# Two layers written out one after the other, and the last stage's constants loaded inside the last layer

## The chip, the cores and the metric

The kernel runs on one core of a Trainium2 chip. The metric is the device time of one execution in microseconds. The core has five engines that run their own instruction streams and meet only at semaphores: TensorE (PE, with its weight loads shown as PEld), VectorE (DVE), ScalarE (ACT), GpSimd (POOL) and SyncE (SP), which here issues nearly all of the transfers.

## The reference, cut to what matters

```python
x = x + gnn(layernorm(x), edge_index)            # two layers, below; 1250 nodes, 512 features
x = x + ffn(layernorm(x))                        # the last stage
# gnn, for l in range(2):
q, k, v = (x @ Wq[l].T + bq[l]) * DH**-0.5, x @ Wk[l].T, x @ Wv[l].T       # 8 heads of 64
w = softmax over the edges of each target of (q[tgt] . k[src])
x = batchnorm(x + (sum of w * v[src]) @ Wo[l].T + bo[l], g1[l], beta1[l])
x = batchnorm(x + relu(x @ W1[l].T + b1[l]) @ W2[l].T + b2[l], g2[l], beta2[l])
# after the two layers: layernorm(x, ln_g, ln_b)
# ffn: four nibbles and three flags of each row are read off, three small two-layer networks
# (160 wide; only 5 rows of w1 and one column of w2 matter) give a number from 0 to 15 for
# each of two nibbles, and a one-hot of it, times 2, is added to columns 80 to 111.
```

## The kernel before, in words

**The first stage** (up to 217 us) normalises the input, counts the edges between every pair of nodes with one-hot products, and stores the logarithm of the counts as a bias, the residual and the shifted input to HBM. It is not touched.

**The layers** are one hardware loop, `with nc.Fori(0, LAYERS) as layer` (L557), so that both run the same instructions; only the transfers use the loop's register, to find their layer's weights. A layer has three blocks, and all five engines meet at the end of each block. The first block (L621) transposes the weights and computes k, q and v. Every float32 operand of a product is split into a high part (`..._hi`, rounded to the type in which TensorE is fast) and a low part (`..._lo`, the rest), and a product is three matmuls. The second block (L743) is the attention. The third (L959) is the output projection, the normalisation `t1`, the small feed-forward network (products called `f` and `g`), and the normalisation `t2`. Its result `t2` is kept feature-major, [128, 4, 1250], so that chunk c holds 128 features.

**The end of a layer.** TensorE does the twelve `g` products (four chunks of three), and after the last of them 70 small matmuls of `keep_clock` (L1033), whose results nobody reads: they are there to keep TensorE's clock up. ScalarE copies each product from PSUM to `t2` (L1070). VectorE takes the moments (L1105, L1100, L1101), waits for ScalarE's square root (L1044), works out scale and shift in five one-column steps (`normed`, L1123 to L1127) and applies them to the chunk (L1129). Then ScalarE makes `h_hi` (L1050), GpSimd makes `h_lo` of the first three chunks (L951, called at L980) and VectorE that of the last one (L1170). `h_hi` and `h_lo` are what the next layer's projections read. SP loads the next layer's Wk at the block's start (L964) and stores each finished chunk of `t2` as the next layer's residual (L968). All of this is done in both passes of the loop, so in the last layer too, where no layer follows.

**The last stage** (L1231) is one more block. TensorE turns `t2` into ten node-major tiles of 125 nodes (L1399); six of them are normalised by VectorE's statistics (L1470), four by ScalarE's sums (L1326, L1334). VectorE multiplies by the gain (L1444), adds the shifted input `x_in2` (L1453), and normalises again. From there on VectorE reads off the nibbles, TensorE does the twenty hidden rows (L1428), and VectorE weights and sums fifteen of them (L1537) while ScalarE and GpSimd share the other five.

The constants of this stage are fetched and built inside it: `gain_all` (L1235) and `x_in2` (L1238) by SP; then one column of each `w2` as `w_out` (L1242) and one element of each `b2` as `b_out` (L1244), also by SP; five rows of `w1` and the bias as `w_in` by nine small transfers on ScalarE's queue (L1315 to L1317). GpSimd clears `w_all` (L1268) and splits `w_in` into high and low (L1277, L1279), and SP copies the two parts by sixteen small transfers into `w_all` (L1251). TensorE spreads `w_out` over all partitions with one product against ones (L1404), after the last of the ten tiles, and ScalarE copies that to `w_out_all` (L1338) after its sums of squares and before the square root of the second half.

What is in which region of SBUF sets when a constant can be loaded: `x_in2` lies where the output projection's `a_hi` was (region R1), and `w_all`, `w_out` and the others lie in regions that the attention's biases or `t1` used.

## Time and profile before

| | |
|---|---|
| time, median of 3 runs | 1246.8 us (1242.3 to 1251.4) |
| time of the profiled execution | 1250.26 us |
| its span, first to last instruction | 1248.4 us |
| mean granted clock of TensorE | 0.94 of full speed |
| PE, PEld busy | 1074.7 us (86%), 888.3 us (71%) |
| DVE busy | 785.0 us (63%) |
| ACT, POOL busy | 566.1 us (45%), 436.9 us (35%) |

The span is the time between the first and the last instruction that the profiler recorded; the device time has 1.9 us around it. The shares are means over the whole run. The stages follow each other with a meeting of all engines between them, so what ends a stage has to be read from that stage alone, from the timeline of each engine. TensorE's granted clock is at 1.0 (2.4 GHz) or 0.5 (1.2 GHz).

### The profile page before, as it was taken

How to read it: one execution, taken by the hardware profiler on the slowest of the kernel's cores; microseconds unless marked ns; L12 is line 12 of the kernel's file. 1: busy time of each engine (PE TensorE's matmuls, PEld its weight loads, DVE VectorE, ACT ScalarE, POOL GpSimd, SP SyncE). 2: the span in 40 equal slices, each digit the busy share in tenths (PEclk: the TensorE clock that was granted, in tenths of full speed). 3: DMA queues.
4: the chain of work that ended last, by engine and by line, in shares of the span. 5: the costliest groups of instructions: out<-in, count | busy, mean ns of one | idle time of the engine just before them, and what ended most of it. 6: DMA issues, size and time to landing. Idle time of an engine off the chain costs nothing. (4 is left out here: it accounts for less than half of the span.)

```text
span 1248.4 us, 20276 instructions
## 1 busy us (share of the span) xinstructions
PE 1074.7 (86%) x6736; PEld 888.3 (71%) x6737; DVE 785.0 (63%) x2449; ACT 566.1 (45%) x1034; POOL 436.9 (35%) x482
## 2 busy tenths in 40 slices
PE   4778785999589999999899699859999999989933
PEld 2545453898578888888698699648888888879821
DVE  5665563232557777777577524247777777748878
ACT  5432331210356666666524320046666666643435
POOL 5655565000244444444212200124444444302314
PEclk9888897999889999999999899889999999999965
DMA  6010124734841212213200454563121211230153
GB/s 129 21 40 20 40 90 125 179 83 93 214 100 34 55 38 51 50 34 116 76 27 21 132 124 103 104 180 79 34 54 34 63 42 34 100 101 1 62 115 85
DMA packets 58472, 96.35 MB, mean 77 GB/s; under 512 B 15874, under 2 KB 39174, under 8 KB 58128
## 3 DMA queue, kind: packets, MB, share of 16 engines
q1 hardware_dynamic: 58348, 95.19, 30.9%
q8 instruction: 52, 0.85, 0.3%
q14 instruction: 36, 0.29, 0.1%
q10 hardware_dynamic: 36, 0.01, 0.0%
HBM read 37.55 MB, written 24.17 MB: 49 GB/s over the span
## 5 line engine op out<-in xcount | busy, mean ns | idle before, releaser
L786 POOL TENSOR_SCALAR probs<-probs,mass_inv 125x1250 f32<-125x1250 f32 x160 | 210.9, 1319 | 309.2 <-DVE mass_inv L909 309.2
L805 PE MATMUL banks<-k_stack,q_stack 128*125 128x416 f32 (+1 forms) x960 | 299.2, 398 | 12.4 <-DVEq L887 12.4
L870 ACT ACTIVATE probs<-probs,neg_peak 125x1250 f32<-125x1250 f32 x160 | 213.5, 1334 | 153.7 <-DVE neg_peak L923 153.7
L900 DVE CUSTOM_DVE_ANT_0 probs<-banks,scores_bias 125x416 f32<-125x416 f32 (+1 forms) x480 | 267.6, 583 | 24.6 <-PE banks L805 20.2
L819 PE MATMUL banks<-ident,probs 125*125 125x125 f32 x1600 | 260.4, 278 | 26.0 <-POOL probs L786 19.6
L819 PEld LDWEIGHTS banks<-ident,probs 125*125 125x125 f32 x1600 | 242.9, 189 | 49.1 <-POOL probs L786 23.2
L859 ACT ACTIVATE probs_t<-banks 125x500 f32<-125x500 f32 x320 | 152.6, 477 | 130.9 <-PE banks L819 130.8
L833 PE MATMUL banks<-probs_t,v_pair 125*64 125x250 f32 x1600 | 186.2, 379 | 0.9 <-ACT probs_t L859 0.9
L805 PEld LDWEIGHTS banks<-k_stack,q_stack 128*125 128x125 f32 x960 | 147.8, 192 | 40.4 <-issue 26.4
L891 DVE COPY probs_t<-banks 125x500 f32<-125x500 f32 x160 | 108.2, 676 | 74.0 <-PE banks L819 74.0
L475 PE MATMUL banks<-onehot_src,onehot_dst 125*125 125x512 bf16 x540 | 120.5, 387 | 32.9 <-POOL onehot_dst L290 17.5
L833 PEld LDWEIGHTS banks<-probs_t,v_pair 125*64 125x64 f32 x1600 | 107.5, 136 | 54.4 <-ACT probs_t L859 1.3
L403 DVE TENSOR_SCALAR onehot_src<-iota,e_col 125x1250 bf16<-125x1250 f16 x180 | 93.9, 566 | 66.8 <-issue 34.1
L475 PEld LDWEIGHTS banks<-onehot_src,onehot_dst 125*125 125x125 bf16 x540 | 76.2, 157 | 77.5 <-issue 56.3
L290 POOL TENSOR_SCALAR onehot_dst<-own,target_col 125x125 bf16<-125x125 f16 x120 | 99.0, 840 | 8.2 <-POOL target_col L287 8.2
L607 POOL CAST q_split<-q_t 128x250 fp32r<-128x250 f32 x40 | 15.8, 395 | 239.5 <-DVE q_t L731 149.6
L951 POOL TENSOR_TENSOR h_lo<-t,h_hi 128x1250 fp32r<-128x1250 f32 x12 | 34.5, 2872 | 117.6 <-ACT h_hi L1050 117.6
L694 PE MATMUL banks<-h_hi,wt_hi 128*128 128x416 f32 (+1 forms) x192 | 69.8, 363 | 2.3 <-DVE k_lo L728 2.3
L694 PE MATMUL banks<-h_hi,wt_lo 128*128 128x416 f32 (+1 forms) x192 | 68.8, 358 | 0.0
L694 PE MATMUL banks<-h_lo,wt_hi 128*128 128x416 f32 (+1 forms) x192 | 68.7, 358 | 0.0
L907 DVE TENSOR_SCALAR mass<-mass 125x1 f32<-125x1 f32 x160 | 24.6, 154 | 69.1 <-ACT probs L870 69.1
L333 ACT ACTIVATE more<-banks 125x1250 f32<-125x1250 f32 x10 | 12.1, 1211 | 113.6 <-PE banks L480 113.6
(247 smaller groups left out, 1459.0 us busy)
## 6 DMA issues: line engine op xcount, KB each, us to landing
q_stack<-q_split SPq DMA_DIRECT2D x160, 125.0 KB, 2.4
scores_bias<-edge_bias SPq DMA_DIRECT2D x8, 1171.9 KB
edge_bias<-bias SPq DMA_DIRECT2D x10, 585.9 KB
k_stack<-k_hi SPq DMA_DIRECT2D x16, 312.5 KB, 4.6
k_stack<-k_lo SPq DMA_DIRECT2D x16, 312.5 KB, 5.6
resid<-residual SPq DMA_DIRECT2D x2, 2500.0 KB, 10.1
residual<-t SPq DMA_DIRECT2D x8, 625.0 KB, 2.9
values<-v_stage SPq DMA_DIRECT2D x2, 2400.0 KB
```

Source lines behind the costliest of these rows:

```text
L290: op = nc.gpsimd.tensor_scalar(onehot_dst[:, k, 0:NT], own[:, 0:NT], target_col[:, k:k + 1], None, ALU.is_equal)
L403: op = nc.vector.tensor_scalar(onehot_src[:, k, :], iota[:, :], e_col[:, 1, ds(first + RING * q + k, 1)], None, ALU.is_equal)
L475: last = nc.tensor.matmul(counts[par][:, s:s + w], onehot_dst[:, k, 0:NT], onehot_src[:, k, s:s + w], start=False, stop=True, skip_group_c ...
L694: mm = nc.tensor.matmul(bank[:, 0:sn], w[:, i, c * P:(c + 1) * P], h[:, i, s0:s0 + sn], **edge)
L786: nc.gpsimd.tensor_scalar(probs[:, u % 4, :], probs[:, u % 4, :], mass_inv[:, u % 4:u % 4 + 1], 1.0, ALU.mult, ALU.mult).then_inc(att["pro ...
L805: mm = nc.tensor.matmul(pb[0:NT, t % 5, 0:sn], q_stack[:, n % 2, half, part, tile * NT:(tile + 1) * NT], k_stack[:, head * N + s0:head * N ...
L819: mm = nc.tensor.transpose(pb[0:NT, 5 + t % 2, j * NT:(j + 1) * NT], probs[:, u % 4, (j0 + j) * NT:(j0 + j + 1) * NT], ident[0:NT, 0:NT])
L833: mm = nc.tensor.matmul(pb[half * DH:(half + 1) * DH, 7, 0:GN], v_pair[:, c % 2, j, half * DH:(half + 1) * DH], probs_t[:, n % 2, half, j, ...
L859: nc.scalar.activation(to, of, ACT.Copy).then_inc(att["t_free0"], 1)
L870: nc.scalar.activation(probs[:, u % 4, :], probs[:, u % 4, :], ACT.Exp, bias=neg_peak[:, u % 4:u % 4 + 1], accum_out=mass[:, u % 4:u % 4 + ...
L891: nc.vector.tensor_copy(to, of).then_inc(att["t_free1"], 1)
L900: nc.vector.tensor_tensor_reduce(out=probs[:, slot % 4, s0:s0 + sn], in0=pb[0:NT, t % 5, 0:sn], in1=scores_bias[:, (n % GROUPS) * GROUP + ...
```

## The change

1. `with nc.Fori(0, LAYERS) as layer` becomes `for layer in range(LAYERS)`: the instructions of both layers are written out. The offsets of the transfers become constants.
2. The last layer makes no `h_hi` and `h_lo`, stores no residual and loads no Wk.
3. In the last layer's third block, SP instead issues the gain, the nine transfers of `w_in` (before on ScalarE's queue, in the last stage) and the six of `w_out` and `b_out`; then waits until the output projection is done and issues the four of `x_in2`; then waits for GpSimd's split and issues the sixteen of `w_all`. GpSimd, after its low parts of the rectified values, sets the ones, clears `w_all` when `t1` is no longer read, and splits `w_in`.
4. In the last stage the product that spreads `w_out` stands ahead of tile 6 of the ten, and ScalarE's copy of it comes first of all its work there. The splits, the clearing of `w_all` and these transfers are gone from this stage. `w_all`, `w_in`, `w_in_hi` and `w_in_lo` lie at other addresses.

```diff
-        with nc.Fori(0, LAYERS) as layer:
...
+        w_all = place("w_all", [P, SET, HID], F32R, "RP")
...
+        w_in = place("w_in", [NF, HID], F32, "RV", 2048)
+        w_in_hi = place("w_in_hi", [NF, HID], F32R, "RV", 7936)
+        w_in_lo = place("w_in_lo", [NF, HID], F32R, "RL", 47872)
...
+        for layer in range(LAYERS):
+            last_layer = layer == LAYERS - 1
...
                 def _(sp):
                     clear(sp, [*att.values(), *bias_in, *v_in, *q_in, v_stored])
 
-                    sp.dma_start(w_nat[0][:, :, :], weight(gnn["Wk"], DC)[:, ds((LAYERS - 1) * DC, DC), :]).then_inc(wk_in, 16)
-
-                    for c in range(DC):
-                        sp.wait_ge(oph["t_done"], DC + 1 + c + len(pieces(c)))
-                        sp.dma_start(res_d[:, c, :], t2[:, c, :]).then_inc(res_stored, 16)
-                    sp.wait_ge(wk_in, 16)
+                    one = lambda v: v.rearrange("(a n) -> a n", a=1)
+                    if last_layer:
+                        sp.dma_start(gain_all[:, :], one(gnn["ln_g"]).to_broadcast([NT, D])).then_inc(fin["gain"], 16)
+                        for o, name in enumerate(OPS):
+                            w1, b1 = ffn[name + "_w1"], ffn[name + "_b1"]
+                            cols = slice(o * GE, (o + 1) * GE)
+                            sp.dma_start(w_in[0:2, cols], w1[0:2, :]).then_inc(fin["w"], 16)
+                            sp.dma_start(w_in[2:5, cols], w1[44:47, :]).then_inc(fin["w"], 16)
+                            sp.dma_start(w_in[5:6, cols], one(b1)).then_inc(fin["w"], 16)
+                        for o, name in enumerate(OPS):
+                            with nc.allow_non_contiguous_dma("one column of w2; one element to all"):
+                                sp.dma_start(w_out[:, o * GE:(o + 1) * GE],
+                                             ffn[name + "_w2"][:, RESULT:RESULT + 1].rearrange("n a -> a n")).then_inc(fin["w_out"], 16)
+                                sp.dma_start(b_out[:, o:o + 1], one(ffn[name + "_b2"])[:, RESULT:RESULT + 1].to_broadcast([NT, 1])).then_inc(fin["b_out"], 16)
+                        sp.wait_ge(oph["filled"], max(t for t, job in enumerate(ojobs) if job[0] == "o") + 1)
+                        for k in range(2):
+                            for rows in SPREAD:
+                                sp.dma_start(x_in2[rows, part(k), :], shifted_d.rearrange("(t p) d -> p t d", p=NT)[rows, part(k), :]).then_inc(fin[f"x{k}"], 16)
+                        sp.wait_ge(fin["w_split"], 2)
+                        sp.wait_ge(fin["consts"], 2)
+                        for q in range(SET):
+                            for k, weights in enumerate((w_in_hi, w_in_lo, w_in_hi, w_in_lo)):
+                                rows = slice(q * ROW + k * NF, q * ROW + (k + 1) * NF)
+                                sp.dma_start(f32(w_all[rows, q, :]), f32(weights[:, :])).then_inc(fin["w_all"], 16)
+                    else:
+                        sp.dma_start(w_nat[0][:, :, :], weight(gnn["Wk"], DC)[:, ds((layer + 1) * DC, DC), :]).then_inc(wk_in, 16)
+
+                        for c in range(DC):
+                            sp.wait_ge(oph["t_done"], DC + 1 + c + len(pieces(c)))
+                            sp.dma_start(res_d[:, c, :], t2[:, c, :]).then_inc(res_stored, 16)
+                        sp.wait_ge(wk_in, 16)
...
                     for n in range(3):
                         pool.wait_ge(oph["done"], ojobs.index(("f", 1, n)) + 1)
                         rectified_low(nc.gpsimd, 1, n)
-                    for c in range(DC - 1):
-                        low(pool, nc.gpsimd, c, t2, h_hi, h_lo, "h_hi", "h_lo")
-                    pool.wait_ge(oph["h_lo"], DC - 1)
+                    if last_layer:
+                        nc.gpsimd.memset(one_f[:, :], 1.0).then_inc(fin["consts"], 1)
+                        pool.wait_ge(oph["h1_lo"], DC - 1)
+                        pool.wait_ge(oph["h1_lo_last"], 2)
+                        pool.wait_ge(oph["h1_hi"], DC + 1)
+                        nc.gpsimd.memset(f32(w_all[:, :, :]), 0.0).then_inc(fin["consts"], 1)
+                        pool.wait_ge(fin["w"], 16 * 9)
+                        nc.gpsimd.tensor_copy(w_in_hi[:, :], w_in[:, :]).then_inc(fin["w_split"], 1)
+                        pool.wait_ge(fin["w_split"], 1)
+                        nc.gpsimd.tensor_tensor(w_in_lo[:, :], w_in[:, :], f32(w_in_hi[:, :]), ALU.subtract).then_inc(fin["w_split"], 1)
+                    else:
+                        for c in range(DC - 1):
+                            low(pool, nc.gpsimd, c, t2, h_hi, h_lo, "h_hi", "h_lo")
+                        pool.wait_ge(oph["h_lo"], DC - 1)
...
                             if c and n == 2:
                                 root(1, c - 1)
-                            if c > 1 and n == 2:
+                            if c > 1 and n == 2 and not last_layer:
                                 high(1, c - 2, h_hi, t2)
                             summed(c, n)
-                    high(1, DC - 2, h_hi, t2)
+                    if not last_layer:
+                        high(1, DC - 2, h_hi, t2)
                     root(1, DC - 1)
-                    high(1, DC - 1, h_hi, t2)
+                    if not last_layer:
+                        high(1, DC - 1, h_hi, t2)
...
                     normed(1, DC - 1, t2, G2, BE2)
-                    low(dve, nc.vector, DC - 1, t2, h_hi, h_lo, "h_hi", "h_lo_last")
+                    if not last_layer:
+                        low(dve, nc.vector, DC - 1, t2, h_hi, h_lo, "h_hi", "h_lo_last")
...
             @block.scalar
...
+                act.wait_ge(fin["w_out_sent"], 1)
+                nc.scalar.activation(w_out_all[:, :], pb[0:NT, 7, 0:HID], ACT.Copy).then_inc(fin["w_out_all"], 1)
                 for i in SPANS[1]:
...
                 op.then_inc(fin["first_squares"], 1)
-                act.wait_ge(fin["w_out_sent"], 1)
-                nc.scalar.activation(w_out_all[:, :], pb[0:NT, 7, 0:HID], ACT.Copy).then_inc(fin["w_out_all"], 1)
                 root(0, 1)
...
             @block.tensor
             def _(pe):
                 for i in range(TILES):
+                    if i == SPANS[1][0]:
+                        pe.wait_ge(fin["w_out"], 48)
+                        pe.wait_ge(fin["consts"], 1)
+                        nc.tensor.matmul(pb[0:NT, 7, 0:HID], one_f[:, :], w_out[:, :], start=True, stop=True).then_inc(fin["w_out_sent"], 1)
                     if i >= 7:
                         pe.wait_ge(fin["used"], i - 6)
                     for c in range(DC):
                         mm = nc.tensor.transpose(pb[0:NT, i % 7, c * P:(c + 1) * P], t2[:, c, i * NT:(i + 1) * NT], ident[:, :])
                     mm.then_inc(fin["turned"], 1)
 
-                pe.wait_ge(fin["w_out"], 48)
-                pe.wait_ge(fin["consts"], 1)
-                nc.tensor.matmul(pb[0:NT, 7, 0:HID], one_f[:, :], w_out[:, :], start=True, stop=True).then_inc(fin["w_out_sent"], 1)
                 pe.wait_ge(fin["used"], TILES)
 
```

## Rows read from the trace of the kernel before

**Rows 1.** Busy time by window: us, then each engine's busy us, PEclk, DMA share, GB/s.
```profile
217.71:702.57 484.86, 452.81 (x2976) 388.73 (x2976) 306.94 (x973) 231.50 (x414) 146.70 (x129) 0.98 0.32 79
706.50:1190.35 483.85, 452.45 (x2976) 388.39 (x2976) 306.98 (x973) 231.41 (x414) 146.54 (x129) 0.97 0.31 77
```

**Rows 2.** The chain that ended last, last stage: start us, us, what.
```profile
1201.25 10.31 DMA w_out<-in_L_ffn_xor_w
...
1211.60 1.97 PE banks L1404 x2
```

**Rows 3.** Instructions of L557 and L1127: ns least/median/most, first and last start.
```profile
L557 PEldq COMPARE_BRANCH  x2: 74/1708/3342, 703.1 to 1190.9; - x2
...
L1127 DVE SCALAR_TENSOR_TENSOR tiny<-mv,tiny,vec x16: 219/221/2506, 643.0 to 1185.6; 128x1 f32<-128x1 f32 x16
```

**Rows 4.** Timeline: the loop's way back, and the second layer's first Exp.
```profile
701.04 1.53 DVE L951 TENSOR_TENSOR h_lo<-t,h_hi 128x625 fp32r<-128x625 f32 x2 [0.28 <-ACT h_hi L1050]
...
706.43 1.28 ACT L712 ACT_TABLE_LOAD   x1 [4.81 <-issue]
706.50 3.67 PE L679 MATMUL banks<-ident,wk_nat 128*128 128x128 f32 x16 [9.43 <-issue]
...
808.23 1.35 ACT L870 ACTIVATE probs<-probs,neg_peak 125x1250 f32<-125x1250 f32 x1 [51.39 <-DVE neg_peak L923]
```

**Rows 5.** VectorE's timeline at the end of the last layer.
```profile
1173.46 2.51 DVE L1127 SCALAR_TENSOR_TENSOR tiny<-mv,tiny,vec 128x1 f32<-128x1 f32 x1
...
1180.07 2.15 DVE L1127 SCALAR_TENSOR_TENSOR tiny<-mv,tiny,vec 128x1 f32<-128x1 f32 x1
...
1185.60 1.78 DVE L1127 SCALAR_TENSOR_TENSOR tiny<-mv,tiny,vec 128x1 f32<-128x1 f32 x1
1187.42 1.12 DVE L1129 TENSOR_SCALAR t<-t,tiny 128x625 f32<-128x625 f32 x2
```

**Rows 6.** GpSimd's timeline in the last layer's third block.
```profile
1160.85 1.07 POOL L956 TENSOR_TENSOR r_lo<-r_full,r_hi 128x416 fp32r<-128x416 f32 x1 [1.09 <-DVE r_full L1157]
1173.04 2.92 POOL L951 TENSOR_TENSOR h_lo<-t,h_hi 128x1250 fp32r<-128x1250 f32 x1 [11.12 <-ACT h_hi L1050]
```

**Rows 7.** TensorE's timeline: the last layer's end, the last stage's start.
```profile
1177.02 7.82 PE L100 MATMUL banks<-ident 128*128 128x256 bf16 x70
1191.00 6.30 PE L1399 MATMUL banks<-ident,t 128*125 128x128 f32 x28 [6.17 <-PEq L959]
```

**Rows 8.** Busy time by window, columns as in rows 1: TensorE's clock.
```profile
710.00:712.00 2.00, 2.00 (x7) 1.92 (x7) 1.37 (x2) 0.60 (x1) 0.00 (x0) 0.50 1.06 367
...
1106.00:1108.00 2.00, 1.28 (x14) 0.57 (x8) 0.00 (x0) 0.38 (x1) 0.00 (x0) 1.00 0.00 0
...
1195.00:1197.00 2.00, 2.00 (x11) 2.00 (x10) 1.69 (x3) 0.00 (x0) 0.00 (x0) 0.50 1.00 185
```

**Rows 9.** VectorE's timeline in the last stage.
```profile
1192.25 0.70 DVE L1470 BATCH_NORM_STATS2 f_st<-banks 125x6 f32<-125x512 f32 x1 [1.90 <-PE banks L1399]
1193.10 0.70 DVE L1470 BATCH_NORM_STATS2 f_st<-banks 125x6 f32<-125x512 f32 x1 [0.15 <-PE banks L1399]
...
1202.47 1.06 DVE L117 TENSOR_SCALAR f_w<-f_w 125x6 f32<-125x6 f32 x1
...
1206.00 0.75 DVE L1453 SCALAR_TENSOR_TENSOR x_res<-x_res,f_w,x_in 125x512 f32<-125x512 f32 x1 [2.27 <-DMA x_in<-shifted]
...
1214.30 0.18 DVE L114 RECIPROCAL f_w<-f_w 125x4 f32<-125x4 f32 x1 [1.26 <-ACT f_w L1321]
```

**Rows 10.** GpSimd's timeline in the last stage.
```profile
1190.98 1.69 POOL L1268 MEMSET w_all<- 128x1920 f32 x1
...
1202.30 1.20 POOL L1279 TENSOR_TENSOR w_in_lo<-w_in,w_in_hi 6x480 fp32r<-6x480 f32 x1
```

**Rows 11.** SP's queue in the last stage, first and last of sixteen.
```profile
1205.06 3.95 SPq L1251 DMA_DIRECT2D w_all<-w_in_hi  x1
...
1218.94 0.66 SPq L1251 DMA_DIRECT2D w_all<-w_in_lo  x1
```

128 lines of the change are left out of this document (47 added, 81 removed).

## The prediction

> **What bounds the kernel now.** I read the windows by stage first. The two passes of the loop take 484.9 and 483.9 us with the same counts of instructions on every engine [rows 1]: 78% of the span, and the change leaves their insides alone but for the last pass's end. So the gain or loss has to come from three seams: the way back of the loop, the end of the last layer, and the last stage. For these I read the chain of waits and then each engine's timeline, because at a meeting of all engines only the latest one counts.
>
> The chain of the last stage goes through the third `w_out` transfer (10.31 us from issue to landing) and the product that spreads it, 1.97 us [rows 2]. VectorE's timeline adds what the chain doesn't show: it waits 2.27 us for `x_in2` and 1.26 us for ScalarE's root, which sits behind the copy of the spread `w_out` [rows 9]. Before the stage, VectorE holds the last layer open; TensorE ends its clock-keeping at 1177.02 + 7.82 = 1184.84 [rows 7], 5.5 us before VectorE's end at 1190.35 [rows 1].
>
> **Writing out the loop.** At the way back, TensorE's branch takes 3.34 us, at the exit, not taken, 0.07 [rows 3]. From the end of VectorE's work (701.04 + 1.53 = 702.57) to the first transpose, 706.50, it is 3.93 us [rows 4]; at the exit, from 1190.35 [rows 1] to 1191.00 [rows 7], 0.65. The difference, **3.3 us**, lies on the path: ScalarE resumes at 706.43 too, and every product of the layer follows. Which value straight code gives is not in these rows. If fetching new code is what costs, and not the branch, nothing is saved; the lower bound is 0. But the first pass is code that has never run, and it is no slower than the second by more than 1.0 us in 484 [rows 1], so I take 3.3. The upper bound adds the clock: in 710 to 712 TensorE still runs at 0.5 [rows 8], that is 1.2 GHz, at half pace since 706.50; were all of these 5.5 us at full clock, 2.75 more would be saved. I expect no such thing, as the idle stretch shortens by 3.3 us only, from 9.43 [rows 4] to about 6.1, and the one of 6.17 us in front of the last stage also ends at 1.2 GHz [rows 7, 8].
>
> The Trainium skill's page "Runtime: NRT & Kernel Launch" (Instruction fetch mechanics) says that fetching ahead is sequential, that crossing a block of code is mostly hidden, and that a taken branch out of the window waits for a fetch. By it the whole 3.3 us goes; by the branch's row alone, anything from 0 to 3.3. No run here yet shows straight code at this seam.
>
> A side effect: ScalarE reloads its function table at the start of the pass, 1.28 us, beside TensorE's first transposes. Without the loop that load can be left out there and fall in front of the first Exp. There ScalarE has been idle for 51.39 us [rows 4], so 0 is likely; if the load waits for the same semaphore as the Exp, it costs at most 2 x 1.28 = 2.6 us over both layers.
>
> **The end of the last layer.** The dropped high parts take ScalarE out of the way, and the dropped low parts take GpSimd out of VectorE's: L1127 is a one-column step of 0.22 us [rows 3], but three times it takes 2.51, 2.15 and 1.78 us [rows 5]. The first ends at 1173.46 + 2.51 = 1175.97, GpSimd's `h_lo` at 1173.04 + 2.92 = 1175.96 [rows 5, 6]: it stands still until GpSimd is done. The three excesses are 6.44 - 0.66 = 5.8 us, all in VectorE's row towards the end. VectorE's last useful step ends at 1187.42 + 1.12 = 1188.54; less 5.8 that is 1182.8. Then TensorE's 70 clock-keeping products, untouched, end last: 1184.84. The stage starts **5.5 us** earlier, not 7.5: the clock-keeping is late next.
>
> What moves in here has to fit. GpSimd is free at 1160.85 + 1.07 = 1161.9 [rows 6] and needs 1.69 for clearing `w_all` and 1.20 for the low part [rows 10]; with the small cast and the ones I put 4 us: done at 1166. VectorE may stand still for at most the 1.20 us, twelve microseconds ahead of TensorE's last real product and at a time when it waits for products anyway: 0. SP's twenty transfers ahead (gain, nine `w_in`, six `w_out` and `b_out`, four `x_in2`) go out during the output projection, where SP before issued only Wk and residuals; they are queued behind nothing that others wait for. Behind the wait for the split stand sixteen `w_all`: the first took 3.95 us, the last 0.66 [rows 11], together 3.95 + 15 x 0.70 = 14.5 us, so SP ends at 1180.5, 4.3 us ahead of TensorE. The Wk load and the four residual stores are worth 0: SP is not the last.
>
> The Trainium skill's page "SBUF — State Buffer" (SBUF: two separate sides) says that a VectorE instruction with two SBUF inputs waits for a GpSimd instruction that reads SBUF, and one with a single input outside the two-port modes never does. By it the moved cast and subtraction may meet only small steps here; the three long L1127 agree with the first half, and no row here tests the second.
>
> **The last stage.** VectorE's row is followed, with what each wait becomes:
> - The first 28 transposes take 6.30 us at 1.2 GHz, 0.225 each [rows 7, 8], and the first six statistics go at their pace: 0.85 apart (1192.25 to 1193.10) for 0.70 us of work [rows 9]. Now the idle time of TensorE before them is about half a microsecond, and across a comparable seam at 1106 to 1108, where it also stood still in part, the clock stayed at 1.0 [rows 8]. At 2.4 GHz four transposes take 0.45, so VectorE's own 0.70 is the pace: 5 x 0.15 = 0.75, 0.4 at the first one, and up to 0.4 more as neighbours overlap. I take 1.5.
> - L117 takes 1.06 us where a like step (L114) takes 0.18; it ends with GpSimd's subtraction, 1202.30 + 1.20 = 1203.50 [rows 9, 10], which has left the stage: 0.9.
> - `x_in2` has landed: 2.27 less an ordinary 0.04, 2.2.
> - The root no longer waits for `w_out`: 1.26 less 0.04, 1.2. The spreading product, 1.97 us at 1.2 GHz [rows 2], about 1.0 at full clock, now stands ahead of tile 6; ScalarE has slack, since tiles 7 to 9 wait for VectorE's multiplications anyway.
>
> Together **5.8 us**. After that VectorE works without a gap through the nibbles, the weighting and the output, and none of it changes.
>
> **The sum.** 3.3 + 5.5 + 5.8 = 14.6 us off 1250.26, the profiled execution's own time: 1235.7. That execution lies 3.5 above the median of the runs, 1246.8; off that, **1232 us**. One percent, 12.5 us, is about what a measurement can tell from no change; the line to "faster" is 1234.3.
>
> **The rivals.**
> - *Straight code stalls as the branch did.* Then only 11.3 is saved: 1235.5. For it: the code is fetched over the same transfer engines. Against: the equal passes. 0.13.
> - *SP becomes the last at the layer's end.* Its sixteen small transfers would need over (1184.8 - 1166) / 16 = 1.2 us each; at 3.95 each, as the first one, it would end 63 us after 1166, but that one stood behind much larger traffic. At 1.5 each SP ends at 1190 and the 5.5 is gone: 1237.5. 0.08.
> - *TensorE's clock has fallen at the seam after all.* The 1.5 of the first item is lost: 1233.5. 0.07.
> - *The table load lands in front of the Exps*: 1234.8. 0.06.
> - *Slower.* Written out, the last pass's code is new, where the loop had it run before. If TensorE then stands still for a branch's 3.34 us at each seam of both layers (three blocks each, six times), 20 us are added against 11.3 saved: 1255.5. It decides from the fourth such stall. The first pass's equal time speaks strongly against it. 0.04.
>
> The forecast keeps 0.62. The range takes the unknown 2.75 of the clock below, and above it the case of straight code that stalls and the SP case, with some 2 us for medians of few runs: 1227 to 1239. Faster by over 1%: nearly all of the forecast's own chance (0.57), most of the clock case and about half of the code and table cases, 0.72; within 1% 0.24; slower 0.04.
>
> **What would show it.** In the profile after: the gap between VectorE's last step of layer one and the first Wk transpose at 0.65 us rather than 3.93; no L951 in the last layer, and three L1127 of 0.22 us there; the last stage's first transpose within a microsecond of the clock-keeping's end; PEclk 1.0 during the 28 transposes and statistics about 0.62 to 0.70 apart; no wait of L1453 on a transfer; the sixteen `w_all` issues over before the clock-keeping ends. It is wrong if the layers' insides grow, if any engine other than TensorE ends the last layer, or if the clock reads 0.5 over the first tiles.

## The result, and the profile after

The changed kernel takes **1235.4 us** (median of 4 runs, 1230.3 to 1236.2) where the kernel before takes 1247.8 (4 runs, 1242.3 to 1251.4). The ratio of the runs is 0.990, with a 95% interval of 0.985 to 0.994: 12.4 us less, 1%. The forecast was 1232, so the time lies 3.4 us above it and inside the range of 1227 to 1239. The profiled execution took 1236.21 us with a span of 1234.5; against the profiled execution of before, 1250.26, that is 14.05 us less, and the forecast's sum was 14.6.

The first part of the page of the kernel after has each engine's busy time, share of the span and number of instructions:

```profile
PE 1072.8 (87%) x6736; PEld 886.3 (72%) x6737; DVE 775.1 (63%) x2447; ACT 561.2 (45%) x1029; POOL 429.4 (35%) x479
```

All five fell a little (VectorE by 9.9 us), and none of that says where 14 us of span went. As before, the seams have to be read. Busy time by window, columns as in [rows 1]: the first layer, from its first Wk transpose to VectorE's last step; the second, from its first transpose to the end of the clock-keeping; then two stretches over the first tiles of the last stage.

```profile
218.81:705.61 486.80, 453.99 (x2976) 389.15 (x2976) 306.86 (x973) 231.36 (x414) 146.53 (x129) 0.97 0.32 79
706.00:1182.80 476.80, 451.97 (x2976) 388.32 (x2976) 299.33 (x971) 226.73 (x409) 141.34 (x130) 0.98 0.33 78
1182.00:1184.00 2.00, 1.58 (x15) 1.28 (x13) 0.08 (x1) 0.00 (x0) 0.83 (x3) 1.00 0.00 0
1184.00:1188.00 4.00, 3.69 (x25) 2.67 (x24) 3.97 (x11) 0.84 (x2) 0.14 (x2) 1.00 0.00 0
```

The first layer is 486.80 us long, where it took 484.83 from the first transpose at 217.74: 1.97 more, with the same number of instructions as in [rows 1]. The last two rows have TensorE's clock at 1.00, 2.4 GHz, where [rows 8] had 0.50 in the same place.

**The loop's seam.** TensorE's timeline at the end of layer one and the start of layer two (start us, us, engine, line, instruction, and in brackets the idle time before it and what ended it); VectorE's last step of layer one stands in the fence after it:

```profile
706.00 3.65 PE L736 MATMUL banks<-ident,wk_nat 128*128 128x128 f32 x16 [6.02 <-PEq L1016]
```

```profile
704.08 1.53 DVE L1008 TENSOR_TENSOR h_lo<-t,h_hi 128x625 fp32r<-128x625 f32 x2 [0.28 <-ACT h_hi L1143]
```

704.08 + 1.53 = 705.61, so TensorE starts 0.39 us behind VectorE, where it was 3.93 [rows 4]. Its idle stretch is 6.02 us, not 9.43, and the sixteen transposes still take 3.65 us, at 1.2 GHz. Behind them the clock came back sooner than before. Busy time over the first six microseconds of layer two, the kernel before and then the kernel after:

```profile
706.50:712.50 6.00, 6.00 (x24) 5.88 (x25) 2.77 (x4) 3.61 (x5) 0.00 (x0) 0.50 1.01 337
```

```profile
706.00:712.00 6.00, 6.00 (x28) 5.95 (x29) 2.76 (x4) 2.39 (x4) 0.00 (x0) 0.66 0.64 176
```

The mean clock is 0.66 where it was 0.50: the stretch at half clock ends 4.1 us behind the first transpose, where it ended 6.0 us behind it.

**The end of the last layer.** L1127 of before is L1222 after. VectorE's timeline:

```profile
1171.42 0.22 DVE L1222 SCALAR_TENSOR_TENSOR tiny<-mv,tiny,vec 128x1 f32<-128x1 f32 x1
...
1179.42 0.22 DVE L1222 SCALAR_TENSOR_TENSOR tiny<-mv,tiny,vec 128x1 f32<-128x1 f32 x1
1179.67 1.12 DVE L1224 TENSOR_SCALAR t<-t,tiny 128x625 f32<-128x625 f32 x2
```

VectorE is done at 1180.79. GpSimd's and SP's timelines there:

```profile
1162.27 1.22 POOL L1070 TENSOR_TENSOR w_in_lo<-w_in,w_in_hi 6x480 fp32r<-6x480 f32 x1
```

```profile
1163.52 0.82 SPq L1044 DMA_DIRECT2D w_all<-w_in_hi  x1
...
1174.28 0.66 SPq L1044 DMA_DIRECT2D w_all<-w_in_lo  x1
```

SP issued its last of the sixteen at 1174.94, and TensorE, on its timeline, ends last:

```profile
1174.98 7.82 PE L100 MATMUL banks<-ident 128*128 128x256 bf16 x70
1183.21 2.86 PE L1409 MATMUL banks<-ident,t 128*125 128x128 f32 x24 [0.42 <-PEq L1016]
```

From the end of the clock-keeping, 1182.80, to the first tile it is 0.41 us; before it was 1191.00 - 1184.84 = 6.16 [rows 7].

**The last stage.** VectorE's timeline, to hold against [rows 9]:

```profile
1183.92 3.69 DVE L1477 BATCH_NORM_STATS2 f_st<-banks 125x6 f32<-125x512 f32 x6 [3.13 <-PE banks L1409]
...
1192.83 0.17 DVE L117 TENSOR_SCALAR f_w<-f_w 125x6 f32<-125x6 f32 x1
...
1193.24 0.75 DVE L1460 SCALAR_TENSOR_TENSOR x_res<-x_res,f_w,x_in 125x512 f32<-125x512 f32 x1
...
1200.18 0.17 DVE L114 RECIPROCAL f_w<-f_w 125x4 f32<-125x4 f32 x1
...
1204.57 0.19 DVE L114 RECIPROCAL f_w<-f_w 125x6 f32<-125x6 f32 x1 [0.34 <-ACT f_w L1327]
```

Six statistics run in one piece, no step waits for a transfer or for ScalarE's square root in the first normalisation, and L117 is short. From the first tile to the reciprocal of the second norm it is 1204.57 - 1183.21 = 21.36 us. The chain of waits of the kernel before has that reciprocal at 1219.04, 28.04 us behind its first tile at 1191.00 [rows 7]. From there to VectorE's last operation both kernels need the same (25.44 and 25.42).

**The accounts** of the profiled executions, by such marks in both traces:

| stretch | before | after | difference |
|---|---|---|---|
| start of the program to the first Wk transpose | 217.74 | 218.81 | +1.07 |
| layer one, to VectorE's last step | 484.83 | 486.80 | +1.97 |
| seam of the loop | 3.93 | 0.39 | -3.54 |
| layer two, to the end of the clock-keeping | 478.34 | 476.80 | -1.54 |
| from there to the first tile | 6.16 | 0.41 | -5.75 |
| last stage to the reciprocal of the second norm | 28.04 | 21.36 | -6.68 |
| the rest of the span | 29.4 | 29.9 | +0.6 |
| sum | 1248.4 | 1234.5 | -13.9 |

The three seams gave 15.97 us; 3.6 came back in places that the change does not touch, and 1.5 went there. The first stage is the least steady of all: over the fourteen profiles of this case it ends between 213.5 and 219.1 us, so that the time of a single execution says little about an edit worth 2 us. Marks inside the stage that was edited do.

Of the 0.6 us in the last row 0.5 is no scatter. From VectorE's last step to the end of the span it is 3.45 us in the kernel before and 3.98 in the kernel after, and 3.4 to 3.5 or 3.9 to 4.0 in every other profile, the larger value in all ten kernels whose last layer makes neither high nor low parts. What takes that half microsecond was not looked into.

### The profile page after: what moved, and what is told of

Same layout as the page of the kernel before. It is cut to its first block and busy times, and to the rows that moved or that the text cites. A ratio compares the mean times of both kernels' runs of the same rounds, so it can differ in the third digit from the quotient of the medians.

```text
span 1234.5 us, 20192 instructions
## 1 busy us (share of the span) xinstructions
PE 1072.8 (87%) x6736; PEld 886.3 (72%) x6737; DVE 775.1 (63%) x2447; ACT 561.2 (45%) x1029; POOL 429.4 (35%) x479
## 5 line engine op out<-in xcount | busy, mean ns | idle before, releaser
L1008 POOL TENSOR_TENSOR h_lo<-t,h_hi 128x1250 fp32r<-128x1250 f32 x9 | 26.0, 2887 | 100.8 <-ACT h_hi L1143 100.8
```

## The experiments

All medians in us; the number of runs stands in brackets. Where several were timed, the ratio to the kernel before on the same chip stands with its 95% interval. "One run" is a single profiled execution. Single executions are compared by their marks, not by their times. The first three build the change up from the kernel before, the next three take the changed kernel's clock-keeping apart, and the others follow what was left over.

| run | time | ratio to before |
|---|---|---|
| loop alone | 1246.24 (10 runs) | 0.9983 (0.9970 to 0.9996) |
| + no GpSimd low parts | 1241.59 (one run) | |
| + no high and low parts at all | 1238.12 (4) | 0.9920 (0.9896 to 0.9944) |
| the change | 1235.42 (4) | 0.9896 (0.9850 to 0.9942) |
| the change, keep 50 at the end | 1230.66 (one run) | |
| keep 0 at the end | 1231.03 (one run) | |
| keep 120 at the loop's seam | 1235.63 (one run) | |
| 120 and 50 | 1229.91 (5) | 0.9859 (0.9834 to 0.9885) |
| + queries' copy first | 1232.67 (4) | 0.9868 (0.9839 to 0.9897) |
| 120 and 50, half the store | **1216.68** (5) | 0.9727 (0.9712 to 0.9742) |
| both | 1216.64 (4) | 0.9709 (0.9676 to 0.9742) |
| 120 and 50, 115 and 55 elsewhere | 1233.23 (4) | 0.9865 (0.9850 to 0.9880) |
| the kernel before, again | 1248.44 (one run) | |

### The loop written out, nothing else

```diff
-        with nc.Fori(0, LAYERS) as layer:
+        for layer in range(LAYERS):
```

> The kernel before with the layers written out and nothing else changed. Theory (the taken branch costs 3.3 us and straight code costs nothing): from VectorE's last step of layer one to the first Wk transpose 0.4 us as in the changed kernel, not 3.93; the end of the last layer and the last stage as before (6.2 us from the clock-keeping's end to the first transpose, 28 us to the second normalisation's inverse root); time 3 to 5 us below before. Rival (written-out code makes the first layer slower, 486.8 us in the changed kernel against 484.9): the first layer again takes 486.5 or more and the gain is 1 to 2 us only.

The ratio is 0.9983: 2.1 us less, with 0.5 to 3.7 in the interval. TensorE's timeline at the seam of this kernel:

```profile
701.10 3.51 PE L679 MATMUL banks<-ident,wk_nat 128*128 128x128 f32 x16 [5.89 <-PEq L959]
```

The seam from VectorE's last step is 0.39 us, so 3.5 us went there. In the same execution layer one was 487.19 us long, 2.4 more than before, and the gain is about 2 us: the marks that the rival named. Not all of this length is the stall that is taken up below. Busy time of this kernel, 23 us into layer one:

```profile
236.80:243.50 6.70, 6.17 (x18) 5.89 (x19) 3.86 (x7) 2.62 (x6) 0.00 (x0) 0.50 0.61 132
```

TensorE is at half clock for 6.8 us there, where it is for 3.4 in both profiles of the kernel before and in every other one but that with clock-keeping at the two other seams. Its projections end 95.43 us behind the first transpose instead of 93.98. The profiled execution is also the fastest of the ten, 1243.43 us, because its first stage, which no edit touched, ended at 213.5 us and not at 217.7.

### GpSimd's low parts of the last layer left out

```diff
-                    for c in range(DC - 1):
-                        low(pool, nc.gpsimd, c, t2, h_hi, h_lo, "h_hi", "h_lo")
-                    pool.wait_ge(oph["h_lo"], DC - 1)
+                    if layer < LAYERS - 1:
+                        for c in range(DC - 1):
+                            low(pool, nc.gpsimd, c, t2, h_hi, h_lo, "h_hi", "h_lo")
+                        pool.wait_ge(oph["h_lo"], DC - 1)
```

> As the kernel with the layers written out alone, but in the last layer GpSimd leaves out its three low parts; ScalarE's high parts and VectorE's own low part of the last chunk stay. Theory (VectorE stands still for GpSimd): the three steps of 1.8 to 2.5 us fall to 0.22, VectorE's last low part ends within 0.5 us of the clock-keeping's end, and the last stage starts 5 to 5.7 us earlier after the clock-keeping than in the kernel with written-out layers alone. Rival (ScalarE's high parts delay the chain): the start moves by less than 2 us.

VectorE's timeline of this kernel, where L1128 is the L1127 of before:

```profile
1179.38 0.22 DVE L1128 SCALAR_TENSOR_TENSOR tiny<-mv,tiny,vec 128x1 f32<-128x1 f32 x1
1179.63 1.12 DVE L1130 TENSOR_SCALAR t<-t,tiny 128x625 f32<-128x625 f32 x2
1181.03 1.53 DVE L951 TENSOR_TENSOR h_lo<-t,h_hi 128x625 fp32r<-128x625 f32 x2 [0.28 <-ACT h_hi L1051]
1183.70 3.69 DVE L1471 BATCH_NORM_STATS2 f_st<-banks 125x6 f32<-125x512 f32 x6 [1.14 <-PE banks L1400]
```

VectorE itself still makes its own `h_lo` here, and yet the first tile starts 0.41 us behind the clock-keeping, as in the full change. GpSimd's three instructions alone had kept VectorE 5.5 to 5.8 us behind; VectorE ends at 1182.56, 0.02 us ahead of TensorE. The last row shows something else: six statistics in 3.69 us, as in the full change. The last stage starts at full clock with this edit, before any constant was moved.

### The high parts and VectorE's low part left out as well

```diff
-                            if c > 1 and n == 2:
+                            if c > 1 and n == 2 and layer < LAYERS - 1:
                                 high(1, c - 2, h_hi, t2)
...
-                    low(dve, nc.vector, DC - 1, t2, h_hi, h_lo, "h_hi", "h_lo_last")
+                    if layer < LAYERS - 1:
+                        low(dve, nc.vector, DC - 1, t2, h_hi, h_lo, "h_hi", "h_lo_last")
```

> Written-out layers and a last layer without any high and low parts; the constants of the last stage are loaded inside it as before. Theory: clock-keeping ends last, the first transpose follows 0.4 us later at full clock, so the start is 5.75 us earlier; but in the stage the w_out transfer, issued from the stage's start, still lands about 20 us into it, so of the 6.7 us that the changed kernel gained there only the faster first transposes show, and they are given back in the wait for the transfers: stage start to inverse root about 28 us. Time 9 to 10 us below before. Rival (the stage's gain came from the clock and not from the constants): 23 us to the inverse root, time 13 us below before.

10.4 us below the kernel before, by medians. TensorE's timeline:

```profile
1170.36 7.82 PE L100 MATMUL banks<-ident 128*128 128x256 bf16 x70
1178.59 3.29 PE L1403 MATMUL banks<-ident,t 128*125 128x128 f32 x28 [0.42 <-PEq L959]
```

VectorE was done at 1176.18, 2.0 us ahead of TensorE, and the seam is the same 0.41 us: leaving out more than GpSimd's parts bought nothing at that seam. From the first tile to the second norm's reciprocal this kernel takes 27.65 us, the kernel before 28.04 and the full change 21.36. The tiles are at full clock (28 transposes in 3.29 us, not 6.30 [rows 7]), but the constants are still late, and VectorE waits for them instead:

```profile
1193.58 0.75 DVE L1457 SCALAR_TENSOR_TENSOR x_res<-x_res,f_w,x_in 125x512 f32<-125x512 f32 x1 [3.90 <-DMA x_in<-shifted]
```

That wait was 2.27 us in the kernel before [rows 9], and one of 0.99 us for the gain is new. The loop alone takes 27.53 us and the second run of the kernel before 27.63, both with an idle stretch of about 6 us in front of the stage, so the full clock by itself shows no gain. So in the last stage the early constants are worth 6.3 us behind a fast clock, and the clock is worth nothing without them. The forecast had added the two as 1.5 and 4.3.

### Fifty clock-keeping products at the end instead of seventy

```diff
-                    keep_clock(len(ojobs) % 8, 70)
+                    keep_clock(len(ojobs) % 8, 50 if last_layer else 70)
```

> The changed kernel with 50 clock-keeping products in the last layer in place of 70. Theory (they are what ends the layer): TensorE is done 2.2 us earlier, VectorE (2.0 us ahead of it in the changed kernel) ends last, the stage starts 2.0 us earlier, and the clock stays at full over the first transposes because TensorE idles for well under a microsecond. Rival: the clock reads half over the first tiles and 1.5 us are given back there.

VectorE's timeline:

```profile
1175.87 0.22 DVE L1222 SCALAR_TENSOR_TENSOR tiny<-mv,tiny,vec 128x1 f32<-128x1 f32 x1
1176.12 1.12 DVE L1224 TENSOR_SCALAR t<-t,tiny 128x625 f32<-128x625 f32 x2
1178.35 3.69 DVE L1477 BATCH_NORM_STATS2 f_st<-banks 125x6 f32<-125x512 f32 x6 [1.10 <-PE banks L1409]
```

The stage starts at 1177.63, behind VectorE's end at 1177.24 and no longer behind the products' at 1177.05, and it is as short as with 70 (21.38 us). That the products were late next is confirmed; about 2 us lay in them (from VectorE's end to the first tile it is 0.39 us, with 70 products 2.42). The time of this one execution, 4.8 us below the change's median, is no measure of it: its first stage was 3.6 us shorter than in the change's profile.

### No clock-keeping at the end

```diff
-                    keep_clock(len(ojobs) % 8, 70)
+                    if not last_layer:
+                        keep_clock(len(ojobs) % 8, 70)
```

> The changed kernel without any clock-keeping products at the end of the last layer (70 before). Theory: VectorE ends the layer as it does with 50 products, 6.3 us after TensorE's last real product, but TensorE has then idled for about 6.7 us and runs the first tiles of the last stage at half clock; the stage takes 1 to 2 us more up to the inverse root of its second normalisation than the 21.4 us it took with 70 and with 50. Rival (the products buy nothing here): 21.4 us again.

Busy time by window, at the start of the last stage, and VectorE's timeline:

```profile
1176.00:1178.00 2.00, 1.30 (x6) 1.33 (x7) 0.38 (x2) 0.00 (x0) 0.97 (x4) 0.50 0.00 0
1178.00:1180.00 2.00, 2.00 (x11) 2.00 (x11) 1.69 (x3) 0.00 (x0) 0.00 (x0) 0.50 0.04 8
```

```profile
1177.93 0.70 DVE L1478 BATCH_NORM_STATS2 f_st<-banks 125x6 f32<-125x512 f32 x1 [1.62 <-PE banks L1410]
1178.78 0.70 DVE L1478 BATCH_NORM_STATS2 f_st<-banks 125x6 f32<-125x512 f32 x1 [0.15 <-PE banks L1410]
...
1180.49 1.89 DVE L1478 BATCH_NORM_STATS2 f_st<-banks 125x6 f32<-125x512 f32 x3 [0.15 <-PE banks L1410]
```

The clock is at 0.50 for the first four tiles and the old pace of 0.85 us is back for three of them; the stage takes 22.65 us instead of 21.36. So the clock-keeping buys 1.3 us in this stage.

### A hundred and twenty products at the loop's seam

```diff
-                    keep_clock(len(ojobs) % 8, 70)
+                    keep_clock(len(ojobs) % 8, 70 if last_layer else 120)
```

> The changed kernel with 120 clock-keeping products at the end of the first layer in place of 70 (the last layer keeps 70). Theory: TensorE idles for 0.8 us instead of 6.0 at the seam of the layers, so the second layer's first transposes and products run at full clock; from the first transpose to the end of the second layer's projections it takes 1.5 to 2 us less than 90.2 us. Rival (the transposes are paced by ScalarE and VectorE, 0.85 us each at half clock and 0.69 at best): under 1 us is gained.

TensorE's timeline at the seam:

```profile
706.71 1.94 PE L736 MATMUL banks<-ident,wk_nat 128*128 128x128 f32 x16 [0.56 <-PEq L1016]
```

The sixteen transposes take 1.94 us instead of 3.65. From the first transpose of layer two to the end of the projections it is 89.19 us instead of 90.35: 1.16 less, between the two expectations. The transposes alone gain 1.71; the other 0.55 is waited away later. The written-out loop alone could not bring this: it left an idle stretch of 6.02 us, and TensorE restarts at half clock behind it.

### Both: 120 at the seam, 50 at the end

```diff
-                    keep_clock(len(ojobs) % 8, 70)
+                    keep_clock(len(ojobs) % 8, 50 if last_layer else 120)
```

> The changed kernel with 50 clock-keeping products in the last layer and 120 in the first. Theory: 2.0 us at the last layer's end and 1.5 to 2 us at the seam of the layers, 3.5 to 4 us below the changed kernel (1235.4), so about 1231.5 and 1.3% below the kernel before. Rival (what the seam gains is lost again in the attention, whose length differs by 2 to 3 us from run to run): 1233.5 or more.

1229.91, 5.5 us below the change by medians; by the ratios, whose intervals overlap (0.9834 to 0.9885 against 0.9850 to 0.9942), about 4.6. Both effects are in the trace: transposes of 1.94 us at the seam, and a last stage that starts 0.58 us after the last product and takes 21.37. This version is the base of the four that follow.

### The queries' copy ahead of the values' store

In all the kernels so far the first layer's length scatters, by 2.6 us from the shortest to the longest, and most of what scatters is one stall. Early in each attention block GpSimd may not split the fourth pass's queries until the copy of the third pass's (`q_stack`) has landed, and SP issues that copy behind the store of all values, 1250 x 512 numbers of four bytes. What GpSimd does next, the normalising of `probs`, waits behind the split, and TensorE waits for that. TensorE's and GpSimd's timelines of the changed kernel, and SP's:

```profile
348.94 1.20 PE L876 MATMUL banks<-ident,probs 125*125 125x125 f32 x4 [9.17 <-POOL probs L843]
```

```profile
346.49 0.39 POOL L664 CAST q_split<-q_t 128x250 fp32r<-128x250 f32 x1 [10.21 <-DMA q_stack<-q_split]
```

```profile
322.32 7.72 SPq L819 DMA_DIRECT2D values<-v_stage  x2
332.92 7.20 SPq L676 DMA_DIRECT2D q_stack<-q_split  x4
```

TensorE stands still for 9.17 us and restarts at half clock. The edit issues the copy first:

```diff
                     bias_part(2 * GROUP, 3 * GROUP)
+                    stacked(sp, 2)
                     for rows in SPREAD:
                         sp.dma_start(v_d.rearrange("(t p) d -> p t d", p=NT)[rows, :, :], v_stage[rows, :, :]).then_inc(v_stored, 16)
-                    stacked(sp, 2)
```

> As e8, but at the start of each attention SP issues the third pass's queries before it stores the values to HBM (2.5 MB), not after. In the changed kernel GpSimd stands still for 10.2 us in each attention for that transfer, TensorE for 9.2 us behind it, and the time TensorE's clock takes to come back afterwards (1 to 6 us over the profiles so far) is what made the first layer of the changed kernel 2 us longer. Theory: the stall shrinks to under 3 us in both layers, the layers' lengths stop differing, and the time falls by 12 us or more below e8. Rival (the transfer engines are full with the values and biases either way, and ScalarE then waits for the stored values instead): the stall moves and less than 5 us are gained.

TensorE's and GpSimd's timelines:

```profile
363.58 1.20 PE L876 MATMUL banks<-ident,probs 125*125 125x125 f32 x4 [10.24 <-POOL probs L843]
```

```profile
361.05 0.39 POOL L664 CAST q_split<-q_t 128x250 fp32r<-128x250 f32 x1 [12.85 <-DMA q_stack<-q_split]
```

TensorE's stall moved by one pass: it starts at 353.3 us, not at 339.8, and did not shrink; the ratio, 0.9868, is that of the base, 0.9859. The order was not the cause: the next small copy then stands behind the same store.

### Half the store

The first two pairs of heads take their values from SBUF (`v_pair` from `v_stage`), so the first half of the stored values is never read. The edit stores the other half only:

```diff
-                        sp.dma_start(v_d.rearrange("(t p) d -> p t d", p=NT)[rows, :, :], v_stage[rows, :, :]).then_inc(v_stored, 16)
+                        sp.dma_start(v_d.rearrange("(t p) d -> p t d", p=NT)[rows, :, 4 * DH:], v_stage[rows, :, 4 * DH:]).then_inc(v_stored, 16)
```

> As e8, but the attention stores only the half of the values to HBM that is ever read back (features 256 to 511; the first half goes to v_pair straight from v_stage): 1.25 MB instead of 2.5. The output stays the reference's. Theory (GpSimd's and TensorE's stall of 9 to 10 us at the start of each attention is the time the third pass's queries spend behind this store): the stall falls to 4 to 6 us in each layer, 8 to 10 us in all, so about 1221. Rival (the store's rows get half as long, and its time goes by their number, not by bytes): the stall stays above 8 us and the time within 2 us of e8's 1229.9.

1216.68, **13.2 us** below its base by medians, 13.1 by the spans of the profiled executions, 16.5 by the ratios (the two were timed on different chips); more than any of the expectations. TensorE's, GpSimd's and SP's timelines, and the windows behind the stall:

```profile
340.38 0.70 PE L876 MATMUL banks<-ident,probs 125*125 125x125 f32 x4 [2.77 <-POOL probs L843]
```

```profile
337.94 0.39 POOL L664 CAST q_split<-q_t 128x250 fp32r<-128x250 f32 x1 [3.82 <-DMA q_stack<-q_split]
```

```profile
320.25 6.90 SPq L819 DMA_DIRECT2D values<-v_stage  x2
330.76 2.44 SPq L676 DMA_DIRECT2D q_stack<-q_split  x4
```

```profile
342.00:352.00 10.00, 10.00 (x77) 7.68 (x76) 7.13 (x26) 5.84 (x12) 4.45 (x5) 1.00 0.61 136
```

The stall fell from 9.38 to 2.77 us in layer one, and the clock did not fall behind it, where the base had 6.0 us at half clock, which cost 3.0. Together 6.6 + 3.0 = 9.6; the layer is 9.4 shorter (486.9 to 477.5). In layer two the stall fell from 8.21 to 3.80 and the time at half clock stayed (3.4 and 3.3): 4.4, and the layer is 4.2 shorter. The two layers add up to 13.6 us, and the rest of the span differs by 0.5 the other way. The rival, by which the store's time goes by the number of its rows, is out: their number stayed and their length was halved. Whether the copy waits for the bytes ahead of it on its queue, or for a share of transfer engines that are busy with all of the traffic (94% from 330 to 340 us in the changed kernel, with the loads of the bias among it), no run separates.

### Half the store, and the queries' copy first

> The half store and, as in e10, the third pass's queries issued ahead of it. In e10 the stall came one pass later, 10.2 us, behind the same store. Theory: with half of it, what is left of the stall is under 3 us per layer and the kernel is 2 to 6 us below e11. Rival (the fourth pass's queries wait as long as the third's did): the same time as e11.

The two edits above, together. 1216.64, the same as without the new order. GpSimd waits 0.92 us where it waited 3.82, but 4.64 at the next split. TensorE's stalls are 2.09 and 4.18 us in the two layers, against 2.77 and 3.80. Order and size were two explanations of one stall, and size is the one that holds.

### Clock-keeping at the two other seams

```diff
-                keep_clock(0, 30)
+                keep_clock(0, 115)
...
-                    keep_clock(len(jobs) % 8, 12)
+                    keep_clock(len(jobs) % 8, 55)
```

> As e8, with 115 clock-keeping products at the end of the first stage (30 before) and 55 at the end of each layer's projections (12 before). Theory: both layers' projections and both attentions start at full clock; about 1 us at the first transposes, 0.5 to 1 us at each attention's start, 2 to 3 us below e8. Rival (those stretches are paced by transfers and by VectorE's 0.58 us per block of scores): within 1 us of e8.

The ratio is 0.9865 against the base's 0.9859: no gain. The first layer's sixteen transposes now take 1.94 us (217.41 to 219.35) where the changed kernel needs 3.47, the mean clock is up from 0.951 to 0.956, and layer one is 488.0 us long, 1.1 more than in the base. TensorE's timeline shows where the gain went:

```profile
241.98 0.71 PE L751 MATMUL banks<-h_hi,wt_hi 128*128 128x416 f32 x1 [4.41 <-DVE k_lo L785]
```

That wait for VectorE was 2.75 us in the changed kernel, and behind it TensorE is now at half clock for 6.8 us, not 3.4. The projections end 96.23 us behind the first transpose, where they end at 94.34 in the base. The faster transposes ended in a longer wait, and that wait cost clock. A higher clock where VectorE or a transfer ends last is not time.

### The kernel before, once more

> The kernel before once more, for its first layer. Theory (the first layer's length is the looped code's or the written-out code's alike, and differs with how long TensorE's clock takes to come back after the stall at the attention's start): it is between 484.7 and 487.6 us, as in the eight profiles of written-out code, and where it is long the clock is at half for longer after the stall. Rival (looped code is faster inside): 484.8 again, with the attention at 295.7.

One run, 1248.44 us. Its marks: layer one 484.99, seam 4.05, clock-keeping's end to the first tile 6.21, last stage to the second norm's reciprocal 27.63. The seams of before repeat within 0.12 us and the last stage within 0.4 from one execution to the next; the changes read there are 3.5 to 6.7 us. Layer one, 484.99 us, lies inside the theory's range and is also what the rival foretold, so this run does not decide between them.

## Why the prediction was right, and what it missed

**Writing out the loop (3.3 forecast): 3.5.** The seam is 0.39 to 0.40 us in every kernel with written-out layers. The lower bound of 0, in which new code has to be waited for, is ruled out at this seam. The upper bound added the clock's 2.75 us, of which the forecast expected nothing. Over the transposes that was right, and only 120 products that filled the gap brought them to 1.94 us. Behind them it was not. In the six kernels with written-out layers and 70 products the half clock ends 2.7 to 4.1 us behind the first transpose of layer two, in the two profiles of the loop 6.0 and 5.7 us. From that transpose to the first score product it is 97.2 to 97.6 us in those six, 98.45 and 98.34 with the loop. So the shorter idle stretch brought about 0.9 us more, inside layer two. The Trainium skill's page "Runtime: NRT & Kernel Launch" (Instruction fetch mechanics) says that a taken branch to code outside of what was fetched ahead stalls, and straight code mostly does not; by it the branch's 3.34 us [rows 3] go, and they did. That they were a fetch, and not another cost of the loop's branch, no run shows.

**The table load (0 forecast): 0.** It left the loop's start and stands in front of the Exps. ScalarE's timeline in layer one of the kernel after:

```profile
320.47 1.28 ACT L927 ACT_TABLE_LOAD   x1 [48.24 <-PEq L678]
323.91 1.34 ACT L927 ACTIVATE probs<-probs,neg_peak 125x1250 f32<-125x1250 f32 x1 [2.16 <-DVE neg_peak L980]
```

It runs as soon as the block starts, and ScalarE still waits 2.16 us for the maximum after it (2.12 in layer two): hidden in full.

**The end of the last layer (5.5 forecast): 5.75.** The argument was that GpSimd's low parts hold three small VectorE steps, and that the clock-keeping is late next. Leaving out GpSimd's instructions alone gave the full amount, and 50 products instead of 70 showed that the products ended last. Layer one of the changed kernel still has GpSimd's low parts, and its longest L1222 is still as long:

```profile
L1222 DVE SCALAR_TENSOR_TENSOR tiny<-mv,tiny,vec x16: 218/219/2516, 646.0 to 1179.4; 128x1 f32<-128x1 f32 x16
```

Most is 2.516 us, least 0.218; in the last layer all are 0.22. The Trainium skill's page "SBUF — State Buffer" (SBUF: two separate sides) says that such a step with two inputs from SBUF and a GpSimd instruction that reads SBUF shut each other out; these runs agree. It frees one-input steps only outside the two-port modes, and the kernel before has rows on both sides of that. GpSimd's and VectorE's timelines:

```profile
1184.55 2.82 POOL L951 TENSOR_TENSOR h_lo<-t,h_hi 128x1250 fp32r<-128x1250 f32 x1 [2.34 <-ACT h_hi L1050]
```

```profile
1185.30 0.27 DVE L1126 TENSOR_SCALAR tiny<-tiny,vec 128x1 f32<-128x1 f32 x1
```

L1126, with one input, ran through inside GpSimd's subtraction in its usual 0.27 us, and L1127 right behind it stood still [rows 5]. But L117 has one input too, six columns wide, and it stood still until the subtraction of `w_in_lo` had ended [rows 9, 10]. The prediction says that no row tests the second half; these do. In which mode L117 ran the trace does not tell.

SP had a wider margin than forecast: it ended at 1174.94, 7.9 us ahead of TensorE instead of 4.3. The first `w_all` transfer took 0.82 us to issue, not 3.95 [rows 11], with the four of `x_in2` issued 23 us ahead of it, at 1139.16, and not right in front of it as in the last stage; GpSimd was also done at 1163.49 instead of 1166.

**The last stage (5.8 forecast): 6.7.** A sum whose terms came out near, and one term missing. From the first tile to the end of the sixth statistic it is 4.40 us instead of 6.22, so the clock gave 1.8 where the forecast had 1.5: the first statistic starts 0.5 sooner behind its tile, and the pace is 3.69 / 6 = 0.61 us instead of 0.85. L117 takes 0.17 (0.9 saved, as forecast). `x_in2` is there without a wait (2.2, as forecast), and so is the square root of the second half (1.4 for 1.2). The missing term is VectorE's wait for ScalarE's sums between the reciprocals at 1214.30 and 1219.04, which is gone as well (0.35). Together 6.65. More important than the sizes: the terms were added as if they were independent, and they are not. With the clock but without the constants the stage gained nothing clear of its own spread, since VectorE only reached the waits for the gain and `x_in2` sooner.

**The layers' insides (0 forecast): +1.97 and -1.54, and the start +1.07.** This is what the prediction did not have, and by its own list of signs a growing layer would have shown it wrong. It took the insides of the layers as fixed, from two passes that agreed within 1.0 us [rows 1]. That they agreed was luck: in the kernel before the second pass reaches its first score product 3.3 us sooner than the first does (98.45 and 101.75 us behind the first transpose), and its attention is 2.3 us longer (302.33 and 300.02 us), with a stall of 10.85 us instead of 8.78. So the equal times say nothing of what code costs that has never run. The written-out second layer does: its code is new, and it reaches its first score product sooner than the loop's second pass. The stall behind the store of the values has a length of its own in each execution, and so has the time until the clock is back after it. Busy time over the same ten microseconds, the kernel before and then the kernel after:

```profile
350.00:360.00 10.00, 10.00 (x77) 7.92 (x76) 6.56 (x24) 5.43 (x11) 3.90 (x5) 0.97 0.59 126
```

```profile
350.00:360.00 10.00, 10.00 (x57) 7.95 (x57) 4.12 (x16) 4.85 (x9) 1.85 (x3) 0.75 0.49 109
```

77 products against 57, at a mean clock of 0.97 against 0.75. Taking layer one of the kernel before as the base, 484.83 us, and adding the difference in the stall and half the difference in the time at half clock gives the other lengths:

| layer one of | stall | at half clock | worked out | measured |
|---|---|---|---|---|
| before | 8.78 | 3.2 | (base) | 484.83 |
| before, again | 8.92 | 3.1 | 484.9 | 484.99 |
| loop alone | 9.37 | 4.3 | 486.0 | 487.19 |
| + no GpSimd low parts | 9.59 | 5.9 | 487.0 | 486.97 |
| + no parts at all | 8.02 | 3.7 | 484.3 | 484.72 |
| the change | 9.17 | 6.1 | 486.7 | 486.80 |
| keep 50 | 9.67 | 5.6 | 486.9 | 487.26 |
| keep 0 | 8.83 | 3.2 | 484.9 | 485.05 |
| keep 120 | 10.13 | 5.6 | 487.4 | 487.29 |
| 120 and 50 | 9.38 | 6.0 | 486.8 | 486.92 |

All but one agree within 0.5 us. The exception, the loop alone, is 1.2 us longer, and it has the longer stretch at half clock 23 us into the layer: half of the extra 3.4 us is 1.7. So the +1.97 of the change is a stall 0.4 longer and a clock that came back 2.9 us later, 1.4 + 0.4. In layer two of the change the stall is shorter (10.85 to 10.62, half clock 3.8 to 3.0), 0.6 us, and the half clock at the layer's start is shorter, 0.9: together 1.5 of the 1.54.

**Left open:** whether written-out code makes this stall longer. In layer one both executions of the loop are among the short ones, but so are two of the eight written-out ones in the table (484.72 and 485.05), and none of the edits between them touches the attention. In layer two the loop's stalls, 10.85 and 9.75 us, are among the long ones (8.2 to 10.6 written out). The times of the runs do not settle it. The loop alone should have gained 3.5 at the seam and 0.9 behind it, 4.4 us, and its ten runs have 0.5 to 3.7, so something gave 0.7 us or more back. The kernel without any high and low parts should have gained 10 and did, by medians 10.4 and by the ratio 10.0 (7.0 to 13.0).

**The number.** Against the profiled execution the forecast said 14.6 and 14.05 was measured, as the seams gave 1.4 more and the rest of the run took back 2.1 net (13.9 in the spans). Of the 3.4 us between 1232 and 1235.4, 2.7 come from the last line of the sum: the profiled execution of before lay 3.5 above its median, and the forecast carried that over, but the profiled execution after lies only 0.8 above its own. Three runs whose ends are 9 us apart give no offset of 3.5 that could be relied on.

**The rivals.** Straight code does not stall (seam 0.39 us), SP is not last, the clock did not fall at the last seam (1.00), the table load is hidden, and no seam of the written-out layers shows a stall like the branch's 3.34 us.

## What to carry to other kernels

Read each seam from the engine that ends last and ask for the next one: here GpSimd's 2.9 us instructions held one-column steps of VectorE, and 2 us of clock-keeping products were waiting behind that. Do not add the gains of one chain: time that an earlier step saves in front of a late transfer is waited away again, so price each edit with the others in place and alone. And look at the parts that stay as well as at those that change: the largest gain here, 13 us, more than the whole change, lay in a store of which half was never read, and it was visible in the kernel before as a stall of 9 to 11 us behind one small copy.

## What the runs showed of the hardware that was not expected

- The same stall at the same place cost different clock: after 8.0 to 10.9 us of idleness TensorE ran at half clock for 3.0 to 6.2 us in the kernels above, after 3.80 us for 3.3 us, and after 2.77 us not at all.
- A small copy issued behind a store of 2.56 MB kept its reader waiting for 10.2 us, behind one of 1.28 MB for 3.8 us; putting it ahead only passed the wait on to the next one (12.9 and 4.6 us).
- Writing out a loop moved the function table's load (1.28 us) from the start of each pass to the front of the first Exp, where ScalarE still waited 2.1 us behind it.
- Faster transposes at the start of layer one ended in a longer wait for VectorE (4.41 us instead of 2.75), and TensorE was at half clock for 6.8 us behind it instead of 3.4: the products meant to keep the clock up cost it a little later.
